# First layer's attention of a two-layer Flamingo block: queries on partitions, or keys on partitions

## What is computed

```
x = x + jnp.tanh(g_xattn[0]) * _L0_xattn_ref(_layernorm(x, axis=-1), ctx_2048, ctx_2048)
x = x + jnp.tanh(g_ffn[0]) * _L0_ffn_ref(_layernorm(x, axis=-1), L0_ffn_gate_w, ...)
...
scores = jnp.einsum('bhqd,bhkd->bhqk', q, kj) * SCALE
causal = j0 + k_off > q_idx
scores = jnp.where(causal[None, None], -jnp.inf, scores)
new_m = jnp.maximum(m, scores.max(axis=-1, keepdims=True))
exp_c = jnp.exp(scores - new_m)
out = jnp.einsum('bhqk,bhkd->bhqd', exp_c / exp_c.sum(axis=-1, keepdims=True), vj)
```

## Time and profile before

| | |
|---|---|
| runs | 1554.06, 1554.99, 1561.32 us; median 1554.99 |
| profiled execution | span 1525.3 us from first to last instruction; no time of its own was recorded beside it, the median is 29.7 us above the span |
| layer 0 | from 0 to about 342 us; its batches 1 to 6 take 37.2 to 37.5 us each |
| experts | from about 343 us to 1000 us |
| layer 1 | from there to the end |
| busy over the span | TensorE 86%, VectorE 64%, ScalarE 60%, GpSimd 34% |
| mean granted TensorE clock | 0.939 |

### The profile page before, as it was taken

How to read it: one execution, slowest core, us unless ns; L and a number is a source line. 1 busy time by engine, 2 the same in 40 slices (tenths; PEclk the granted TensorE clock), 3 DMA queues, 4 the chain that set the end, 5 groups by cost and what they waited for, 6 DMA issues and landing times.

```text
span 1525.3 us, 37150 instructions
## 1 busy us (share of the span) xinstructions
PE 1309.4 (86%) x10733; PEld 834.6 (55%) x10734; DVE 972.8 (64%) x2387; ACT 920.1 (60%) x2261; POOL 520.1 (34%) x531
## 2 busy tenths in 40 slices
PE   5888888837999999999999999477989889898984
PEld 3656655524556666665666666144556555555552
DVE  5888888755456665655655633255787777776853
ACT  4777777724556666666666666244766667667661
POOL 1044444455333433332000001665554444541000
PEclk9988888968999999999999999688999999999997
DMA  2044344458888767767676545775654555642000
GB/s 72 29 173 180 146 146 151 156 213 304 269 285 282 256 219 261 238 217 244 218 242 222 181 149 154 126 111 83 98 99 65 104 82 84 100 65 52 15 1 28
DMA packets 96131, 233.39 MB, mean 153 GB/s; under 512 B 11808, under 2 KB 11808, under 8 KB 91424
## 3 DMA queue, kind: packets, MB, share of 16 engines
q0 software_dynamic: 33712, 113.79, 29.8%
q1 hardware_dynamic: 62320, 118.34, 23.3%
HBM read 140.84 MB, written 91.24 MB: 152 GB/s over the span
## 4 chain that ended last, share of the span: by engine, by line
PE 45%; DMA 9%; DVE 9%; issue 8%; ACT 3%; POOL 3%; SPq 1%; DVEq 0%; ACTq 0%; POOLq 0%
PE bank L1305 18%; PE bank L1329 10%; PE bank L1542 6%; DMA xs<-y_tiles,slot_ix 5%; PE bank L1293 4%; PE bank L258 2%; PE bank L1316 1%; PE bank L278 1%; DMA xg<-x_slots 1%; DVE l_nmax L325 1%; PE bank L1548 1%; POOL xs L430 1%; DMA x_slots<-blank 1%; DVE l_stack L379 1%; PE bank L240 1%
## 5 line engine op out<-in xcount | busy, mean ns | idle before, releaser
L1305 PE MATMUL bank<-wh,xT 128*128 x1280 | 343.3, 330 | 4.7 <-DVE hp L1420 4.4
L430 POOL DMA_INDIRECT xs<-y_tiles,slot_ix x120 | 194.6, 1622 | 234.2 <-DMA y_tiles<-ysb 99.1
L293 ACT ACTIVATE l_probs<-bank,l_bias 128x256 f32<-128x256 f32 (+1 forms) x512 | 224.4, 449 | 64.4 <-DVE l_bias L327 64.0
L1305 PE MATMUL bank<-wl,xT 128*128 x640 | 211.4, 330 | 0.0
L325 DVE TENSOR_REDUCE l_nmax<-bank 128x2 f32<-128x512 f32 (+1 forms) x256 | 158.1, 617 | 70.8 <-PE bank L240 41.3
L1410 DVE SCALAR_TENSOR_TENSOR hv<-bank,sg 128x192 f32<-128x192 f32 x160 | 56.9, 356 | 227.5 <-ACT sg L1364 203.5
L1379 ACT ACTIVATE ysb<-bank,xg 128x512 f32<-128x512 f32 x160 | 109.9, 687 | 119.1 <-PE bank L1329 119.1
L305 ACT ACTIVATE l_probsT<-bank 128x512 f32<-128x512 f32 (+1 forms) x256 | 140.0, 547 | 65.6 <-PE bank L278 65.2
L1358 ACT ACTIVATE xT<-bank 128x1024 f16<-128x1024 f16 x160 | 162.5, 1016 | 15.0 <-PE bank L1293 14.8
L1305 PEld LDWEIGHTS bank<-wh,xT 128*128 128x128 f16 x1280 | 126.5, 99 | 81.3 <-issue 11.1
L1329 PE MATMUL bank<-wh,hT 128*128 x480 | 156.1, 380 | 0.9 <-issue 0.9
(11 more groups left out here) (246 smaller groups left out, 2538.1 us busy)
## 6 DMA issues: line engine op xcount, KB each, us to landing
xg<-x_slots SPq DMA_DIRECT2D x160, 272.0 KB, 2.8
y_tiles<-ysb SPq DMA_DIRECT2D x160, 256.0 KB, 2.5
raw<-in_experts_dram POOLq DMA_DIRECT2D x30, 1280.0 KB, 7.1
x_slots<-blank SPq DMA_DIRECT2D x33, 272.0 KB, 3.6
xs<-in_x_dram SPq DMA_DIRECT2D x8, 512.0 KB, 4.4
cbuf<-in_ctx_dram SPq DMA_DIRECT2D x8, 512.0 KB, 5.8
stage<-in_mats_dram POOLq DMA_DIRECT2D x4, 1024.0 KB, 7.8
room<-in_ctx_dram SPq DMA_DIRECT2D x8, 512.0 KB, 4.6
```

The lines of the kernel that those rows point to most:

```text
L293: last = self.nc.scalar.activation(self.probs[:, s % 2, u, 0:nk], self.pS[s % 2][:, u * S : u * S + nk], ACT.Exp, bias=self.bias[:, s % 4, ...
L430: return nc.gpsimd.indirect_dma_start(to, None, self.y_tiles[0 : (MT + 1 - k) * P, :], ix, compute_op=ALU.add)
L1305: last = nc.tensor.matmul(bGU[t.place % 2][:, 0:GU], xT[:, t.place % 2, xo + c * P : xo + (c + 1) * P], wp[:, bass.ds(w, 1), c * GU : (c + ...
```

## The change

Layer 0 uses a new class `KeyMajor` in place of `Attention` (layer 1 keeps the old one). A step is now a pair of heads with all 256 queries, 8 steps (`PAIRS`) for a batch.

- Scores are made twice. `pe_max_scores` makes them as before (queries on partitions), for the maxima alone: 128 by 128 and 128 by 256 for each head, in `pA`. VectorE reduces each head's 384 columns to 3 numbers, and for every second pair joins the two parts of the second half, scales by -1/2^18 and splits the result in f16 high and low parts (`mx`).
- `pe_turn_max` transposes `mx`, and ScalarE copies it to SBUF (`mT`): `act_max`.
- `pe_scores` makes the scores again with the keys on partitions, adds the transposed mask, and adds the negated maxima by a product of a selector (`sel`) with `mT`. ScalarE takes `Exp` of 384 columns for each head with no bias and no sum, straight into `probsT`. No transposes of probabilities and no copies of them remain.
- `pe_pv` multiplies V, and beside it a block of ones (`ones32`), with the probabilities; four groups of 32 output partitions hold two heads' results and their sums. ScalarE copies the output four times a batch instead of two; the turning back and the division take four pieces, `o0` to `o3`, each with its own reciprocal.
- The tables are new, the stack pieces use one PSUM bank (`pK`) in the order `BANKS_SEQ`, five are copied by ScalarE and three by VectorE.
- At the start, GpSimd makes two constants, waits for the first norm's variance, and then makes the rest; TensorE does all stack pieces before its first scores. x is loaded two batches ahead.

```diff
-BY_ACT = (1, 5)
+M_POST = 8
-ORDER_PREP0 = ["ln", "c", "S0", "S1", "xn", "S2", "S3", "q", "S4", "S5", "S6", "S7"]
+ORDER_PREP0 = ["ln", "xn", "q", "S0", "S2", "c", "S4", "S6", "S1", "S3", "S5", "S7"]
 PREP0 = dict(
+    pe={3: ["<S0", "S2"], 4: ["<S4", "S6"], 5: ["<S1"], 6: ["<S3"], 7: ["<S5", "S7"]},
+    act={1: ["q"], 3: ["S0", "c"], 4: ["S4"], 5: ["S1"], 6: ["S3"], 7: ["S5"]},
+    pool={0: ["ln"]},
+    dve={0: ["ln"], 1: ["xn"], 2: ["q"], 3: ["c", "S2"], 4: ["S6"], 7: ["S7"]})
 POST0 = dict(
-    pe={0: ["o0"], 2: ["<o1"], 4: ["x0"], 5: ["x1"], 7: ["<g"], 9: ["pos"]},
-    act={3: ["y0"], 4: ["x0", "y1"], 5: ["x1"], 8: ["ex"]},
+    pe={0: ["<o0", "o1"], 1: ["o2"], 2: ["o3"], 3: ["x0"], 4: ["x1"], 5: ["g"], 6: ["pos"]},
+    act={3: ["y0"], 4: ["x0", "y1"], 5: ["x1"], 6: ["ex"]},
+    pool={2: ["pw"]},
+    dve={0: ["o0", "o1"], 1: ["o2", "m0"], 2: ["o3", "m1"], 3: ["n0", "n1"], 4: ["z0"], 5: ["z1", "ra", "rb"],
+         6: ["rc", "rd", "re"], 7: ["rf", "rg"]})
+PAIRS = NH // 2
+BANKS_SEQ = (0, 2, 4, 6, 1, 3, 5, 7)
+BY_DVE = (2, 6, 7)
+class KeyMajor:
+        self.pA, self.pB, self.pO, self.pK = bank[0:2], bank[2:4], bank[4:6], bank[7]
+    def pe_stack(self, pe, b, k):
+        j, half, at = k // 2, k % 2, BANKS_SEQ.index(k)
+        pe.wait_ge(self.parts_ready, 4 * b.n + j + 1)
+        if at > 0:
+            pe.wait_ge(*self.copied(b.n, BANKS_SEQ[at - 1]))
...
+    def pe_max_scores(self, pe, b, j):
+        if j == 0:
+            self.wait_stack(pe, b.n, 0)
+        for u in range(2):
+            if g > 0:
+                pe.wait_ge(self.a_read, 2 * g + u - 1)
+            if u == 1 and g % 2 == 0 and g > 0:
+                pe.wait_ge(self.mT_ready, g // 2)
+            self.nc.tensor.matmul(o[:, 0:P], q[:, 0:P], k[:, 0:P], start=True, stop=False)
+            self.nc.tensor.matmul(o[:, 0:P], self.idb[:], self.maskb[:], start=False, stop=True)
+            self.nc.tensor.matmul(o[:, P : 3 * P], q[:, P:S], k[:, 0:S], start=True, stop=False)
+            self.nc.tensor.matmul(o[:, 2 * P : 3 * P], self.idb[:], self.maskb[:], start=False, stop=True).then_inc(self.a_made, 1)
+    def pe_scores(self, pe, b, j):
+        pe.wait_ge(self.mT_ready, g // 2 + 1)
+        for u in range(2):
+            if g > 0:
+                pe.wait_ge(self.probs_made, 2 * g + u - 1)
+            self.nc.tensor.matmul(o[:, 0:S], k[:, 0:P], q[:, 0:S], start=True, stop=False)
+            self.nc.tensor.matmul(o[:, 0:P], self.idb[:], self.maskT[:], start=False, stop=False)
+            self.nc.tensor.matmul(o[:, 0:S], pick, m[:, 0:S], start=False, stop=True)
+            self.nc.tensor.matmul(o[:, S : S + P], k[:, P:S], q[:, P:S], start=True, stop=False)
+            self.nc.tensor.matmul(o[:, S : S + P], self.idb[:], self.maskT[:], start=False, stop=False)
+            self.nc.tensor.matmul(o[:, S : S + P], pick, m[:, P:S], start=False, stop=True).then_inc(self.b_made, 1)
+    def pe_pv(self, pe, b, j):
+        for kt in range(QT):
+            for part in range(2):
+                for u in range(2):
+                    h, r = 2 * j + u, D * (2 * part + u)
+                    w = self.ones32[:, 0:D] if part else self.v[:, b.par, kt, D * h : D * h + D]
+                    to = o[r : r + D, at + kt * P : at + S]
+    def pe_step(self, pe, b, j, more, before, side):
+        if j % 2 and (j < PAIRS - 1 or more):
+            self.pe_turn_max(pe, (g + 1) // 2)
+        if j + 3 < PAIRS:
+            self.pe_max_scores(pe, b, j + 3)
...
+        side(j, True)
+        if j > 0:
+            self.pe_pv(pe, b, j - 1)
...
+        if j + 1 < PAIRS:
+            self.pe_scores(pe, b, j + 1)
...
+        side(j, False)
+    def act_step(self, act, b, j, more, side):
+        if j % 2 and (j < PAIRS - 1 or more):
+            self.act_max(act, (g + 1) // 2)
+        if j % 2 and j > 1:
+            self.act_out(act, b, (j - 3) // 2)
...
+        side(j)
+        if j + 1 < PAIRS:
+            self.act_exp(act, b, j + 1)
```

More of the change, by code:

```diff
@@ L644, in pe_post0 @@
             else:
-                pe.wait_ge(post_read, 4 * b.n + (1 if piece == "o0" else READ.index(before) + 2))
+                pe.wait_ge(post_read, 6 * b.n + (1 if piece == "o0" else READ.index(before) + 2))
             if piece[0] == "o":
-                t = int(piece[1])
-                pe.wait_ge(at.out_read, 2 * b.n + t + 2)
-                for c in range(HC):
-                    last = nc.tensor.transpose(mPost[:, c * P : (c + 1) * P], at.outT[:, b.par, t, c * P : (c + 1) * P], id32[:])
+                r, t = divmod(int(piece[1]), QT)
+                pe.wait_ge(at.out_read, 4 * b.n + 2 * r + 2)
+                for c in range(4):
+                    first = S * (c % 2) + P * t
+                    last = nc.tensor.transpose(mPost[:, c * P : (c + 1) * P], at.outT[:, 2 * r + c // 2, first : first + P], id32[:])
             elif piece[0] == "x":
@@ L855, in _ @@
             assert n[0] == N_CONST, n[0]
-            b0 = Batch(0, 0, 0)
-            for piece in in_order(PREP["pool"], ORDER_PREP0):
-                pool_prep0(pool, b0, piece)
             sends, SENDS = [0], QT * TOPK
@@ L867, in body @@
             def body(b, prep, post):
-                for s in range(STEPS):
-                    for piece in pieces(POST["pool"], s) if post else []:
+                for j in range(PAIRS):
+                    for piece in pieces(POST["pool"], j) if post else []:
                         pool_post0(pool, b.prev(), piece)
-                    for piece in pieces(PREP["pool"], s) if prep else []:
+                    for piece in pieces(PREP["pool"], j) if prep else []:
                         pool_prep0(pool, b.next(), piece)
-                    ready = SENDS * (b.n - 1 + (s >= FIRST_SEND))
-                    if sends[0] < ready:
-                        pool.wait_ge(at.probs_made, STEPS * b.n + s + 1)
-                        send_next()
+                    ready = SENDS * (b.n - 1 + (j >= FIRST_SEND))
+                    for u in range(2):
+                        if sends[0] < ready:
+                            pool.wait_ge(at.probs_made, 2 * (PAIRS * b.n + j) + u + 1)
+                            send_next()
             over_batches(lambda b: body(b, True, False), lambda b: body(b, True, True), lambda b: body(b, False, True))
@@ L891, in _ @@
                 send_next()
[L892 removed]
+            for n in (12, 14, 16, 18):
                 pool.wait_ge(dve_post, marks + n)
@@ L994, in _ @@
                 dve_prep0(dve, b0, piece, prep)
-            at.dve_max(dve, b0, 0)
-            at.dve_max(dve, b0, 1)
+            dve.wait_ge(consts, N_CONST)
+            dve.wait_ge(gates_ready, 1)
+            for j in range(3):
+                at.dve_max(dve, b0, j)
             def body(b, do_prep, do_post, more):
-                for s in range(STEPS):
-                    at.dve_step(dve, b, s, more, before=do_post)
+                for s in range(PAIRS):
+                    at.dve_step(dve, b, s, more)
                     for piece in pieces(POST["dve"], s) if do_post else []:
@@ L1037, in body @@
                                  lambda piece: pe_prep0(pe, b.next(), piece), lambda piece: pe_post0(pe, b.prev(), piece))
-                for s in range(STEPS):
-                    at.pe_step(pe, b, s, more, before=post, between=lambda: side(s, True))
-                    side(s, False)
+                for j in range(PAIRS):
+                    at.pe_step(pe, b, j, more, post, side)
             over_batches(lambda b: body(b, True, False, True), lambda b: body(b, True, True, True),
@@ L1334, in step @@
             def step(t):
-                code = pe.value_load(t_pe[0:1, t.column()])
+                code = pe.value_load(t_pe[0:1, t.column()], min_val=0, max_val=E * E)
                 e, before = code & (E - 1), code >> 5
@@ L1448, in step @@
             def step(t):
-                code = dve.value_load(t_dve[0:1, t.column()])
+                code = dve.value_load(t_dve[0:1, t.column()], min_val=0, max_val=2**24)
                 with dve.If((code & 1) > 0):
```

269 lines of the change are left out of this document (207 added, 62 removed).

## The result

The change made the kernel slower: 1589.12 us (four runs, 1585.65 to 1594.71) against 1556.29 us (four runs, 1554.06 to 1561.32), ratio 1.0213, 95% interval 1.0183 to 1.0243. The forecast was 1588 us.

What follows compares the result with a forecast made beforehand. VectorE's list (33.2 us a batch) bounded the old kernel; new waits were to make batches 42.2 instead of 37.5: six add 28.2, start and end 4.8, span 1525.3 to 1558, plus 29.7: 1588 us (range 1578 to 1596, whole 1528 to 1612).

Steps and rivals of the forecast that it cites:

- The walk of a steady batch: Layer 0, one batch followed step by step: VectorE 31.0 us of work plus 10.3 idle, 41.3 instead of 37.5.
- exponentials 0.59 us: Sign that the forecast is right: ScalarE's `Exp` of 384 columns takes 0.59 us, extrapolated from 0.367 and 0.478.
- Rival 1: VectorE's list alone decides layer 0 and hand-overs hide: 33.0 us a batch, 1533 us in all; chance 0.27.
- rival 2: Half of the walk's waits in layer 0 vanish: 36.7 us a batch, no change, 1555 us; chance 0.13.
- Rival 3: TensorE slower: low clock to step 5 (45.3 a batch, 1607) or V products not four-way (44.2, 1600); chance 0.22.
- my estimate of 1.1 us: TensorE's product with V for a pair, by the skill's 2.38: about 1.1 us, where the forecast took 0.85.
- The clock's term: TensorE's clock falls in idle stretches; doubling scores(3), 0.9 us, behind the first brings a steady batch to 42.2 us.
- the 45.3 us: Steady batch of layer 0 if TensorE's low clock level holds through step 4: another 3.1 us beyond 42.2.
- TensorE's "28 us": TensorE's sum of work in a layer 0 batch: gains about 1 us, to some 28 us.
- the experts and layer 1 keep their code: The change lies in layer 0, the first 342 us; the rest is unchanged and starts when it ends.
- the median lies 29.7 above that span: Whole kernel: 29.7 us added to the predicted profiled span of 1558 to give the median, 1588 us.
- the sum's +33 for layer 0: Layer 0: +28.2 us from six steady batches and net +4.8 from start, first batch, last batch and last finishing.

Runs made afterwards that it cites:

- after_again: The changed kernel itself, unchanged, run again on chip A: 1572.09 us against 1520.12 for the kernel before, ratio 1.0345.
- q_later: The changed kernel with ScalarE's piece `q` in step 2 instead of step 1: 1558.92 us on chip A, ratio to the kernel before 1.0230.
- s_act: The changed kernel with stack copies `S2` and `S6` moved from VectorE to ScalarE: 1585.15 us on chip A, ratio to the kernel before 1.0424.
- no_ones: The changed kernel without the products with the ones columns from the third batch on: 1573.54 us on chip A, against 1572.09 with them.
- before_bounds: The kernel before with only the bounds on three register loads of the experts added: 1530.93 us on chip A against 1522.10, ratio 1.0044.

## Why the prediction was right, and where it wasn't

**The walk of a steady batch was right**: the places of its waits all, and their lengths to 0.3 us but for `o3`. Predicted and measured (after_again, chip A, us):

| place | predicted | measured |
|---|---|---|
| TensorE ahead of scores(3), through `q` on ScalarE | 3.5 | 3.56 |
| TensorE at `<S0` | 3.0 | 2.76 |
| TensorE at `<S4` | 2.3 | 2.19 |
| VectorE for `o3` | 1.3 | 2.40 |
| VectorE for `c` | 1.8 | 1.61 |
| VectorE for `S6` | 1.4 | 1.32 |
| VectorE ahead of `ra` | 2.7 | 2.64 |
| steady batch | 42.2 | 42.7 |

The trace shows these stretches; q_later shows that one of them is on the path, and s_act that VectorE's sum isn't. (The sign "exponentials 0.59 us" was wrong: 0.49.) **Rival 1** (0.27) and **rival 2** fell by that. **Rival 3** was the slower V product or a lasting low clock. The product took 0.79 us a pair, and no_ones shows that four groups cost no more than two. The Trainium skill ("TensorE: Matmul & The Clock Gate", section "Measured speedup vs the span model") gives 2.38 times for three column tiles, and my estimate of 1.1 us put that number on four groups. By the prediction's own 0.22 us for one stream of 128 columns, 12 of them in 0.79 us is 3.3 times.

**The clock's term has no measurement of its own.** The prediction added 0.9 us, as if only scores(3) ran slowly. But an old batch already spends 10.2 us at the lower level (granted clock 0.86 over the old batch shown with the result), and one of after_again 6.8 to 10.2 us (0.92 to 0.88); the first trace has a batch with 3.4 us of it (0.96) that still takes 41.55. So more time at that level is not what made the batches longer; where it lies goes with about 2 us of one. Steps 4 and 5 of two batches of after_again:

```profile
86.10:95.50 9.40, 7.78 (x110) 6.32 (x108) 6.79 (x15) 6.20 (x13) 0.00 (x0) 0.94 0.00 0
```

```profile
128.30:139.20 10.90, 8.25 (x101) 6.31 (x100) 6.75 (x15) 6.22 (x12) 4.26 (x5) 0.84 0.35 140
```

Both batches spend 10.2 us at the lower level. The first does so in one piece, from 77.1 to 87.3, mostly ahead of step 4; steps 4 and 5 then take 9.4 us and the batch 41.6. The second does so in three pieces of 3.4 us, the last from 131.7 to 135.1, inside these steps; they take 10.9 us and the batch 43.8. The Trainium skill ("TensorE: Matmul & The Clock Gate", section "HAM oscillation — how this bites in real kernels") warns of a loop that idles in every turn. The granted clock does fall one to three times in each batch here, but it did so once in each old one too, and the 45.3 us that I had taken the warning to mean were not reached.

**Off in size**, all from chip A's pair of traces (before_bounds, whose layer 0 is the old one, and after_again): the old batch is 37.5 (as taken), so six steady ones add 31.4 instead of 28.2. The start adds 12.7 (12.3 forecast), the first batch -1.8 (-2.9). From the last batch's first exponentials to the turning of its outputs it is -4.8 (-6.7), and from there to the last product of the tables +4.4 (+2.1); I had counted two more round trips and no more. The first work of the experts comes 1.1 later still. Layer 0 sums to +43, not +33. TensorE's "28 us" was too low: outside its idle stretches it works 32.4 us of a batch, the time at the lower level included. VectorE's list was to lose 2.2 us and lost 1.5 of busy time.

**Two steps failed.** The first: "the experts and layer 1 keep their code". They don't: the three bounds are part of the diff and cost 8.8 us by the medians (3 to 10 by the interval). The second: "the median lies 29.7 above that span". A span lies 1.8 us under its own execution's time. The profiled execution of before (span 1525.3) agrees with chip A (before_bounds: layer 0 ends at 345.54 there, at 345.70 in the trace of before), while the times shown came from a chip on which before takes 1556. On chip A my sum would have said 1527 + 33 = 1560, and 1572 was measured. A third was missized: the sum's +33 for layer 0 measures +43, mostly in the last finishing (+5.5 with the way to the experts against +2.1), the steady batches (+3.2) and the last batch (+1.9).

**So 1588 was met partly by luck.** The change costs 52 us on chip A and 33 on that of the first comparison, and only the second is what the sum said: layer 0 alone takes 43 us more on chip A, and the sum had nothing for the bounds. On chips other than A the engines have unrecorded waits during the sends: the first trace after has them in its last batch (37.5 us of exponentials against 25.7). The experts and layer 1 take the same on all of them: 1180 to 1187 us from the end of layer 0 in the traces of the first comparison, B and C, 1178 to 1187 in those of chip A with the bounds. That points at layer 0 for the 36 us which the kernel before lacks there too. But before was never traced on such a chip, so where it loses them stays open, and with it why the two errors cancel.

## What to carry to other kernels

Where engines run lists in a fixed order, sum each engine's work up to every piece that another waits for, not over the whole loop: the changed kernel took 1.5 us off VectorE's and 7.4 off ScalarE's busy time in a batch, and a batch took 5 us more, and taking more off VectorE lost another 2. Move a blocking wait behind work that is ready (one table entry gave 13 us), and look for what is late next before counting on the whole stretch. Read a diff to its end, and hold a profiled execution against its own time before adding anything for what lies around the span.
